# Whitening stage: the instance gate's small operations placed inside the Gram loop, rest terms of all eight tiles kept

## The reference

```python
x = x + _L1_conv_ref(_gn(x), fc1_w, ln_g, ln_b, fc2_w, x_weight)

def _L1_conv_ref(X, fc1_w, ln_g, ln_b, fc2_w, x_weight):
    x_var = jnp.var(X.reshape(N, C, -1), axis=-1, ddof=1)
    h = x_var @ fc1_w.T                                  # the instance gate: (32, 16)
    h = (h - h.mean(-1)) / jnp.sqrt(h.var(-1) + LN_EPS) * ln_g + ln_b
    y = jax.nn.sigmoid(relu(h) @ fc2_w.T)
    xin = (y / jnp.sqrt(x_var.mean()))[:, :, None, None] * X
    xc = x - x.mean(-1)                                  # x: 4 groups of 16 channels
    Sigma = 1.0 / m * I + EPS * einsum('gdm,gem->gde', xc, xc)   # the Gram matrix
    Sigma_N = Sigma / trace(Sigma)
    P = I
    for _ in range(3):
        P = -0.5 * P + 1.5 * (P @ P @ P @ Sigma_N)
    w = sigmoid(x_weight)
    return w * (P @ x) + (1.0 - w) * xin
```

## Time and profile before

| | us |
|---|---|
| median of 3 runs | 1346.93 |
| lowest and highest run | 1344.14, 1347.83 |
| profiled execution | 1337.93 |
| its span | 1336.1 |
| whitening stage in it (258.7 to 308.7) | 50.0 |

### The profile page before, as it was taken

The page is one execution under the profiler, slowest core; times in us unless marked ns, Lnnn a source line. Parts: engine busy times, 40 slices in busy tenths (PEclk is TensorE's granted clock), DMA queues, the critical chain, the costliest instruction groups (busy, mean ns, idle before and its releaser), DMA issues. The chain is left out here.

```text
span 1336.1 us, 27269 instructions
## 1 busy us (share of the span) xinstructions
PE 1023.1 (77%) x9646; PEld 588.6 (44%) x9646; DVE 846.9 (63%) x2450; ACT 516.2 (39%) x1332; POOL 273.9 (21%) x376
## 2 busy tenths in 40 slices
PE   6878886577888756666666666666973999999996
PEld 2366652253666434454544444443541333333332
DVE  6686746745556465555555555555356788888885
ACT  3543433353443322222223222323542554455452
POOL 4504003200000000000000000000100355555556
PEclk9889998878999955555555555557995999999998
DMA  7000002000000000000000000000001755555550
GB/s 230 1 1 1 1 2 79 0 1 0 1 0 1 1 1 1 0 0 0 0 0 0 0 0 0 0 0 1 0 1 36 170 130 118 124 134 119 119 134 9
DMA packets 10675, 47.39 MB, mean 35 GB/s; under 512 B 1520, under 2 KB 5744, under 8 KB 6128
## 3 DMA queue, kind: packets, MB, share of 16 engines
q1 hardware_dynamic: 10608, 46.49, 14.2%
HBM read 43.86 MB, written 2.62 MB: 35 GB/s over the span
## 5 line engine op out<-in xcount | busy, mean ns | idle before, releaser
L1636 PE MATMUL wide<-ls_h,ls_v 128*128 128x16 f16 x2304 | 105.1, 176 | 145.2 <-DVE ls_h L1735 141.8
L2145 ACT ACTIVATE ex_gated<-wide,unscale 128x1024 f32<-128x1024 f32 x128 | 142.2, 1114 | 139.7 <-PE wide L2111 139.5
L2161 DVE TENSOR_TENSOR ex_hid<-wide,ex_gated 128x1024 f32<-128x1024 f32 x128 | 155.9, 1223 | 39.4 <-ACT ex_gated L2145 28.0
L1636 PEld LDWEIGHTS wide<-ls_h,ls_v 128*128 128x128 bf16 x2304 | 82.0, 106 | 214.2 <-DVE ls_h L1735 214.1
L2087 POOL TENSOR_TENSOR ex_acc<-ex_part,ex_acc 128x512 f32<-128x512 f32 x120 | 152.6, 1272 | 94.7 <-DVE ex_part L2177 80.5
L1725 DVE TENSOR_TENSOR_SCAN ls_cells<-ls_terms 128x48 f32<-128x48 f32 x256 | 73.8, 288 | 123.6 <-ACT ls_terms L1660 123.6
L1660 ACT ACTIVATE ls_terms<-wide 128x32 f32<-128x32 f32 x256 | 54.3, 212 | 229.4 <-PE wide L1641 229.4
L2123 PE MATMUL wide<-ex_hid,w 128*64 128x512 f32 x512 | 116.7, 598 | 0.0
L2111 PE MATMUL wide<-xh,wh 64*128 64x512 f16 x512 | 99.1, 383 | 5.2 <-PEq L81 3.7
L2111 PE MATMUL wide<-xl,wh 64*128 64x512 f16 x512 | 98.3, 380 | 0.0
L2111 PE MATMUL wide<-xh,wl 64*128 64x512 f16 x512 | 98.2, 380 | 0.0
(11 more groups left out here) (368 smaller groups left out, 1882.4 us busy)
## 6 DMA issues: line engine op xcount, KB each, us to landing
ex_d<-route SPq DMA_DIRECT2D x64, 512.0 KB, 6.4
par_attn<-in_attn SPq DMA_DIRECT2D x1, 2704.0 KB, 13.6
par_rest<-in_rest SPq DMA_DIRECT2D x1, 2523.5 KB, 18.9
L_xin<-in_x SPq DMA_DIRECT2D x8, 256.0 KB, 5.7
w<-in_w SPq DMA_DIRECT2D x1, 2048.0 KB, 8.2
out<-ex_acc SPq DMA_DIRECT2D x16, 128.0 KB, 3.3
w<-in_w SPq DMA_DIRECT2D x1, 512.0 KB, 9.1
route<-ro_dt SPq DMA_DIRECT2D x2, 256.0 KB, 2.0
```

The source lines that it names most:

```text
L1636: pe.matmul(ig[:, g, :] if g < 2 else o, vp[part][:, g, :], h1[:], start=False, stop=False, skip_group_check=True)
L2145: act.activation(gated[:, n % 2, :], pair_of_up(n // GS, 2 * (n % GS))[:], ACT.Silu, scale=m.unscale[:, 0:1]).then_inc(s["gated_ready"], 1)
L2161: dve.tensor_tensor(hid[:, n % (2 * GS), :], pair_of_up(n // GS, 2 * (n % GS) + 1)[:], gated[:, n % 2, :], ALU.mult).then_inc(s["hid_ready ...
```

## The change

The stage's arithmetic is the same. What moves is this. DVE's gate operations become three functions: `hidden_gate` (the seven up to the variance) is called in the Gram loop after the iteration i = 1, `normed_gate` (the five up to the relu) after i = 2, and `turned_gate` (the copy of the transposed matrix) after the loop. PE's transpose of the gate is after the matmuls of i = 2, and fc2 after the whole loop, ahead of the closing matmul. ACT's square root and the sigmoid of `x_weight` come after its copies of i = 1, and the gate's own sigmoid after the loop, ahead of the `xn` work. For this the Gram loops of the three engines, and the add and rest loops of DVE and ACT, are written out instead of being hardware loops; PE's apply loop and ACT's `xn` loop stay hardware loops. `rest` has eight tiles, and ACT's wait for `out_ready` is gone.

```diff
-        rest = sb("rest", [P, 4, TW])
+        rest = sb("rest", [P, TILES, TW])
...
-            pe.wait_ge(s["hrelu_ready"], 1)
-            pe.transpose(bank[2][0:2 * HD, 0:HB], h[:, 7, :], p["ident"][0:HB, 0:HB]).then_inc(s["turn_done"], 1)
-            pe.wait_ge(s["ht_ready"], 1)
-            pe.matmul(bank[4][:, 0:HB], p["fc2"][0:2 * HD, :], hT[:], start=True, stop=True)\
-              .then_inc(s["fc2_done"], 1)
...
-            with pe.Fori(0, TILES // 2) as i:
+            for i in range(TILES // 2):
...
+                if i == 2:
+                    pe.wait_ge(s["hrelu_ready"], 1)
+                    pe.transpose(bank[2][0:2 * HD, 0:HB], h[:, 7, :], p["ident"][0:HB, 0:HB])\
+                      .then_inc(s["turn_done"], 1)
+            pe.wait_ge(s["ht_ready"], 1)
+            pe.matmul(bank[4][:, 0:HB], p["fc2"][0:2 * HD, :], hT[:], start=True, stop=True)\
+              .then_inc(s["fc2_done"], 1)
...
-            act.activation(hs[:, 2, :], hs[:, 1, :], ACT.Sqrt).then_inc(s["hstd_ready"], 1)
-            act.activation(scal[:, 1:2], p["x_weight"], ACT.Sigmoid).then_inc(s["sig_ready"], 1)
-            act.wait_ge(s["fc2_done"], 1)
-            act.activation(gate[:], bank[4][:, 0:HB], ACT.Sigmoid).then_inc(s["sig_ready"], 1)
-            with act.Fori(0, TILES // 2) as i:
+            for i in range(TILES // 2):
...
+                if i == 1:
+                    act.wait_ge(s["hvar_ready"], 1)
+                    act.activation(hs[:, 2, :], hs[:, 1, :], ACT.Sqrt).then_inc(s["hstd_ready"], 1)
+                    act.activation(scal[:, 1:2], p["x_weight"], ACT.Sigmoid).then_inc(s["sig_ready"], 1)
+            act.wait_ge(s["fc2_done"], 1)
+            act.activation(gate[:], bank[4][:, 0:HB], ACT.Sigmoid).then_inc(s["sig_ready"], 1)
...
-                    act.wait_ge(s["out_ready"], t + 1)
                     for q in range(2):
                         n = 2 * t + q
-                        act.activation(rest[:, k, q * HW:(q + 1) * HW], m.xa[:, bass.ds(n * HW, HW)], ACT.Identity,
+                        act.activation(rest[:, t, q * HW:(q + 1) * HW], m.xa[:, bass.ds(n * HW, HW)], ACT.Identity,
...
-            with dve.Fori(0, TILES // 2) as i:
+            for i in range(TILES // 2):
...
+                if i == 1:
+                    hidden_gate()
+                if i == 2:
+                    normed_gate()
+            turned_gate()
```

More of the change, by code:

```diff
@@ L996, in _ @@
             act.activation(scal[:, 0:1], bank[3][:, 0:1], ACT.Sqrt).then_inc(s["scale_ready"], 1)
-            act.wait_ge(s["hvar_ready"], 1)
-            act.activation(hs[:, 2, :], hs[:, 1, :], ACT.Sqrt).then_inc(s["hstd_ready"], 1)
-            act.activation(scal[:, 1:2], p["x_weight"], ACT.Sigmoid).then_inc(s["sig_ready"], 1)
-            act.wait_ge(s["fc2_done"], 1)
-            act.activation(gate[:], bank[4][:, 0:HB], ACT.Sigmoid).then_inc(s["sig_ready"], 1)
-            with act.Fori(0, TILES // 2) as i:
+            for i in range(TILES // 2):
                 for k in range(2):
@@ L1013, in _ @@
             act.wait_ge(s["gate_ready"], 1)
-            with act.Fori(0, TILES // 4) as i:
+            for i in range(TILES // 4):
                 for k in range(4):
                     t = 4 * i + k
-                    act.wait_ge(s["out_ready"], t + 1)
                     for q in range(2):
                         n = 2 * t + q
-                        act.activation(rest[:, k, q * HW:(q + 1) * HW], m.xa[:, bass.ds(n * HW, HW)], ACT.Identity,
+                        act.activation(rest[:, t, q * HW:(q + 1) * HW], m.xa[:, bass.ds(n * HW, HW)], ACT.Identity,
                                        scale=ga[:, bass.ds(n, 1)], bias=gb[:, bass.ds(n, 1)])\
@@ L1069, in over16 @@
                 return v.unsqueeze(2).broadcast_to([HB, 2, HD])
[L1071 to L1082, removed]
@@ L1083, in _, with hidden_gate @@
-            link(dve.tensor_tensor(h[:, 5, :], h[:, 4, :], p["ln_b"][0:HB, :], ALU.add))
-            dve.tensor_scalar(h[:, 7, :], h[:, 5, :], 0.0, None, ALU.max).then_inc(s["hrelu_ready"], 1)
-            dve.wait_ge(s["turn_done"], 1)
-            dve.tensor_copy(hT[:], bank[2][0:2 * HD, 0:HB]).then_inc(s["ht_ready"], 1)
+            def hidden_gate():
+                dve.wait_ge(s["fc1_done"], 1)
+                link(dve.tensor_copy(h[:, 0, :], bank[2][0:HB, 0:2 * HD]))
+                link(dve.tensor_reduce(hs[:, 0, :], two(h[:, 0, :]), AXX, ALU.add))
+                link(dve.tensor_scalar(hs[:, 0, :], hs[:, 0, :], 1.0 / HD, None, ALU.mult))
+                link(dve.tensor_tensor(two(h[:, 1, :]), two(h[:, 0, :]), over16(hs[:, 0, :]), ALU.subtract))
+                link(dve.tensor_tensor(h[:, 2, :], h[:, 1, :], h[:, 1, :], ALU.mult))
+                link(dve.tensor_reduce(hs[:, 1, :], two(h[:, 2, :]), AXX, ALU.add))
+                dve.tensor_scalar(hs[:, 1, :], hs[:, 1, :], 1.0 / HD, 1e-5, ALU.mult, ALU.add).then_inc(s["hvar_ready"], 1)
@@ new lines, in normed_gate @@
+            def normed_gate():
+                dve.wait_ge(s["hstd_ready"], 1)
+                link(dve.reciprocal(hs[:, 3, :], hs[:, 2, :]))
+                link(dve.tensor_tensor(two(h[:, 3, :]), two(h[:, 1, :]), over16(hs[:, 3, :]), ALU.mult))
+                link(dve.tensor_tensor(h[:, 4, :], h[:, 3, :], p["ln_g"][0:HB, :], ALU.mult))
+                link(dve.tensor_tensor(h[:, 5, :], h[:, 4, :], p["ln_b"][0:HB, :], ALU.add))
+                dve.tensor_scalar(h[:, 7, :], h[:, 5, :], 0.0, None, ALU.max).then_inc(s["hrelu_ready"], 1)
@@ L1087, in _, with turned_gate @@
+            def turned_gate():
+                dve.wait_ge(s["turn_done"], 1)
+                dve.tensor_copy(hT[:], bank[2][0:2 * HD, 0:HB]).then_inc(s["ht_ready"], 1)
             dve.wait_ge(s["centre_ready"], 1)
-            with dve.Fori(0, TILES // 2) as i:
+            for i in range(TILES // 2):
                 for k in range(2):
@@ L1138, in _ @@
             dve.tensor_scalar(wP[:], pw[:, 0, :], scal[:, 1:2], None, ALU.mult).then_inc(s["wp_ready"], 1)
-            with dve.Fori(0, TILES // 4) as i:
+            for i in range(TILES // 4):
                 for k in range(4):
@@ L1143, in _ @@
                     dve.wait_ge(s["rest_ready"], 2 * t + 2)
-                    dve.tensor_tensor(tile_of(m.xa, t), bank[k + 1][:], rest[:, k, :], ALU.add)\
+                    dve.tensor_tensor(tile_of(m.xa, t), bank[k + 1][:], rest[:, t, :], ALU.add)\
                        .then_inc(s["out_ready"], 1)
```

## The result

The changed kernel takes 1337.82 us, the median of 4 runs (1335.43 to 1342.27), beside 1346.57 for the kernel before (4 runs, 1344.14 to 1347.83). The ratio is 0.9945, with a 95% interval from 0.9922 to 0.9968: 7.4 us faster, between 4.3 and 10.5 (the two medians themselves are 8.75 apart). Forecast were 1345.2 us and a gain of 1.75. The profiled execution of the changed kernel took 1342.27 us with a span of 1340.5; the one of the kernel before took 1337.93. So the two profiles stand in the opposite order to the medians, and that turns out to be the heart of the case.

A forecast was written before the change was run, and what follows sets the result against it. PE and the ACT copy it waits for were taken to pace the Gram loop, with DVE and ACT having holes. -3.25 + 0.1 + 1.4 = -1.75 us gave 1346.93 - 1.75 = 1345.2 us, range 1340.5 to 1348.5.

The forecast's parts named there:

- Head: Whitening stage's start: DVE's centring follows the centred bias directly, at 265.62 instead of 268.87; gain 3.25 us (3.15 to 3.35).
- Gram loop with transpose and tail: PE's transpose inside the loop loses 0.1 us; after it the mask waits for fc2, sigmoid and scaling, losing 1.4.
- Holes: Gram loop: hidden_gate (1.40 us) and normed_gate (1.03) fit DVE's idle 2.15 and 1.87, costing nothing.
- table load: Gram loop: ACT's square root, single load and sigmoid, 1.72 us, fit its 2.17 hole; rival, load too long, 1346.1, chance 0.03.
- rest terms: Apply: ACT's sixteen pieces take 8.1 us without waits, done before the first add; eight buffers gain nothing.
- the last of the prediction's own signs of being wrong: Final item listed as what the profile would show if the forecast were wrong: a difference outside the whitening stage.
- The median lies 9.0 us above that execution: Whole kernel: the -1.75 us was applied to the median 1346.93 as to the profiled 1337.93, giving 1345.2.
- the rival on the clock's dates: Gram loop, apply, later stages: clock rises shift, 0.85 us either way; chances, including unexplained later shifts, 0.18 better, 0.13 worse.

The follow-up runs named there:

- the kernel before run again: The kernel before, no edit, timed against itself: 1347.09 us, ratio 1.0008 (0.9995 to 1.0021).
- the last set: Third of three sets of four kernels, each timed in five rounds beside the kernel before, on another chip than the first two; there the kernel before took 1346.92 us.
- the delay of 1.7 us: The kernel before with eight linked DVE copies added ahead of the centring: 1351.10 us, ratio 1.0026.
- three of the kernels: Kernel before with loops written out and eight rest tiles, 1340.39 us; only its rest/add part, 1343.75; changed kernel with transpose and fc2 moved into PE's holes, 1339.30.
- the filled kernels: Fourteen unused PE matmuls added in idle gaps at slice attention's end: kernel before 1341.42 us, changed kernel 1341.15 us.

## Why the prediction was wrong

**The stage: right.** Head: forecast -3.25; the distance from the centred bias's start to the centring's went from 3.55 to 0.26 (3.54 to 0.26 in the two first traces), 3.3. Gram loop with transpose and tail: forecast +0.1 and +1.4. Against the kernel before run again, with 16.0 us from centring to mask, the 17.5 of the changed kernel are +1.5. The first trace had 15.4, since its clock rose earlier in the loop. Its parts: sigmoid 0.03 after fc2, scaling and mask within 1.3 us of the sigmoid's end, as worked out. Holes, table load, rest terms: right. The drain that the Trainium skill (ScalarE: Activation LUTs, What ACT_TABLE_LOAD costs) adds to a switch of tables isn't there: the next ACTIVATE starts 0.02 after the load's end, as in the earlier trace rows. In the apply the clock's date took 0.7 back: 9.6 us from its start to the last add beside 8.9. Net of the stage: 1.1 against the repeated run of before, 1.75 forecast. Against the first trace it is 1.8, but that agreement is luck: there the loop took 15.4 and the apply 10.3, two dates of the clock that happen to cancel. (The ends of the forecast range, 1340.5 and 1348.5, are each 0.2 above what their terms give, which changes nothing here.)

**The kernel: wrong, by two steps.** What came is the last of the prediction's own signs of being wrong, a difference that lies outside the stage. The first step is the sentence "The median lies 9.0 us above that execution, for which no row has a reason; I carry the difference over to it". There was a reason to look for. The first profile came from an execution unlike most. In the last set 35 executions of the kernel before gave three between 1337.95 and 1339.06 and all others from 1343.39 to 1349.54, and 1337.93 belongs to the three. Over all three sets and the repeat they are four of a hundred (1336.16 to 1339.06), and the other 96 start at 1342.55. Its trace has no fall of the clock between 338 and 470, where the repeated one falls at 446 and 460; that is 5.5 us (3.9 in the slice stretch, 1.6 in the next) towards the 9.3 between the two spans. The attention ahead of the whitening was 4.4 us shorter in it, too, 85.2 beside 89.6 from its first to its last att_yt, with 10.1 us at half clock in it beside 17.9. So the profile showed no cost of the clock after the layer norm, while the repeated trace has it, and the changed kernel is spared part of it. That the typical execution is like the repeated one is read from its time (1347.14, near the median) and not from more traces.

The second is the rival on the clock's dates. It priced them as differences of 1.7 us between two rises, 0.85 us each, and gave them no direction. The rate was about right, half a microsecond for each of half clock: 10.2 us at half clock cost 3.9, so 0.4. Wrong was the size, since a fall in a gap brings a stretch of 10 us, and a second fall behind it; and wrong was the lack of a direction. By its times the kernel before has the falls in most executions, so there was more to win than to lose; the delay of 1.7 us, which left them where they were, lost. The rival also looked for the cause in a shift of some 2 us from the whitening, where three of the kernels got theirs from 0.4 us of DVE's issue in slice attention. By the table, the change's 6.5 us are 1.1 in the stage and 5.4 behind it: 3.2 in slice attention, 1.6 and 1.2 in the stretches with layer norms (the 1.2 not by a fall but by a rise that comes 7.6 instead of 9.3 us after the last LSTM step), against small differences the other way. The time of 1337.82 lies below the range for this reason; some 2 us more of it are scatter between sets, since the same kernel took 1340.21 when it was run again.

**What stays open.** Why DVE's hole is there in one program and not in another: a run that adds instructions to DVE's list without lengthening any path would test it. What sets the clock's dates against the work: the kernel before has the fall in one trace and not in the other, with the same instructions, and for the changed kernel no run separated its earlier rise of the clock from its hole. Nor was it tried to keep PE busy in the last stretch, where the filled kernels differ by 1.6.

## What to carry to other kernels

Before a profile is used for a sum, hold its own time against the median: if they differ by more than the effect in question, the profile may be of another kind of execution, as here, and the prices of the granted clock in it are then not those of the median. List the idle gaps of PE of two or three microseconds in all stages behind the change, not only in the changed one, and see for each whether the clock falls in it; each is a place where half a microsecond of shift can be worth four. When a time moves and the edited stage doesn't, lay two traces side by side from the next stage on and look for the first start that differs: here it was one idle time of 0.3 us on DVE, put down to issue. And where such a gap can't be closed, filling it with matmuls that nobody needs may pay more than tuning what lies before it: here 5.5 us for 14 of them. In a list of one engine, an operation that was early and is now late must be followed to what stands behind it: the scaling ahead of the mask took back half of the head's gain, and moving fc2 by half a loop body gave it back.

## What the runs showed of the hardware

The same idle gap of 3.0 us on PE had a fall of the granted clock in four traces and not in five others, and the gap's place against the last rise differed by only 0.1 us between the two groups (103.79 and 103.88, both of one program). The four falls came 105.8 us after that rise. After a fall 2 us into the gap, the half clock stayed for 10.2 us of dense work; after the one 0.6 us behind the gap in the changed kernel, for 3.4. The second fall of the kernel before, at 459.76, came 0.3 us after an idle time of only 0.78 us on PE, the second of that length since the clock had risen at 456.35. The two profiled executions of the changed kernel had their falls and rises between 320 and 480 us within 0.1 us of one another; the two of the kernel before didn't (falls at 446 and 460 in one, none there in the other), so the dates repeat in some programs and not in all. DVE stood idle for 0.30 to 0.32 us ahead of the first sl_bm in eight traces and not at all in six, and the repeated traces of the kernel before and of the changed kernel agree in it; the profile shows nothing that it waited for. An added 0.6 us of work made the kernel 7.4 us slower, an added 1.7 us on the kernel before 3.5 us slower, and 14 added matmuls 5.5 us faster.
